# The order on TensorE of a fused attention and expert kernel: the two transposes of a chunk put side by side, and the last batch's projection put behind the scores

## What is computed

```python
def _fastmax_causal_p1(q, k, v):
    qn = max over tokens of |q|;  kn = max over tokens of |k|     # one number each for a head
    q = q / qn;  k = k / kn
    kv = jnp.cumsum(k[..., :, None] * v[..., None, :], axis=2)
    num = jnp.cumsum(v, axis=2) + jnp.einsum('bhnd,bhnde->bhne', q, kv)
    ksum = jnp.cumsum(k, axis=2)
    den = jnp.arange(1, n + 1) + jnp.einsum('bhnd,bhnd->bhn', q, ksum)
    return num / den[..., None]

xn = _layernorm(x)
out = x + attention(xn, Wq, Wk, Wv) @ Wo.T + bo + sum of 2 of 8 experts of xn: (silu(xn @ gate) * (xn @ up)) @ down
```

## Time and profile before

| | |
|---|---|
| median of 3 runs | 1246.61 us (1245.76 to 1248.01) |
| profiled execution, its own time | 1249.39 us |
| its span, first to last instruction | 1247.6 us |
| PE busy | 1162.6 us, 93% of the span, 24462 matmuls |
| DVE busy | 900.1 us, 72% |
| ACT busy | 718.6 us, 58% |
| POOL busy | 325.4 us, 26% |
| chain that ended last | PE 81%, DVE 8%, issue 3%, DMA 3%, POOL 3%, ACT 1% |
| mean granted TensorE clock | 0.981 of full speed |

### The profile page before, as it was taken

One profiled execution on the slowest core, in us unless ns is written; L12 is line 12 of the kernel. 1 busy time (PEld: TensorE's weight loads), 2 busy tenths in 40 slices (PEclk: granted clock), 3 DMA queues, 4 the chain that ended last, 5 costly groups with the idle time before them and its releaser, 6 DMA issues.

```text
span 1247.6 us, 58621 instructions
## 1 busy us (share of the span) xinstructions
PE 1162.6 (93%) x24462; PEld 1037.9 (83%) x24463; DVE 900.1 (72%) x2518; ACT 718.6 (58%) x1707; POOL 325.4 (26%) x461
## 2 busy tenths in 40 slices
PE   6899999999999999999999999998979999999990
PEld 5688888878887888888788878887869999999980
DVE  6888778877887887788788778877873444444446
ACT  5666566646765565656476566746544555555550
POOL 4000111111111111111111111231572555555550
PEclk9999999999999999999999999999998999999995
DMA  7000000000000000000000000002245777777779
GB/s 244 1 4 6 12 12 12 14 12 12 15 12 11 15 14 12 12 15 13 12 14 15 12 12 15 14 25 59 72 115 191 263 273 263 272 262 267 268 258 378
DMA packets 59943, 109.40 MB, mean 88 GB/s; under 512 B 9072, under 2 KB 30192, under 8 KB 59728
## 3 DMA queue, kind: packets, MB, share of 16 engines
q1 hardware_dynamic: 49216, 82.80, 19.3%
q0 software_dynamic: 9216, 19.19, 4.7%
q10 hardware_dynamic: 1296, 4.19, 0.8%
HBM read 28.94 MB, written 24.58 MB: 43 GB/s over the span
## 4 chain that ended last, share of the span: by engine, by line
PE 81%; DVE 8%; issue 3%; DMA 3%; POOL 3%; ACT 1%; SPq 0%; POOLq 0%; DVEq 0%; ACTq 0%
PE bank L1250 12%; PE bank L1252 10%; PE bank L1251 10%; PE bank L1536 8%; PE bank L1424 8%; PE bank L1350 6%; PE bank L1402 5%; PE bank L1289 4%; PE bank L1387 4%; PE bank L1376 4%; PE bank L1336 3%; PE bank L1413 2%; DVE qs L850 2%; PE bank L1368 1%; PE bank L1516 1%
## 5 line engine op out<-in xcount | busy, mean ns | idle before, releaser
L1219 DVE TENSOR_TENSOR aT<-bank,aT 128x256 f32<-128x256 f32 (+1 forms) x216 | 91.4, 423 | 148.4 <-ACT aT L771 142.9
L505 POOL COPY xn<-meta 128x2 f32<-128x2 f32 x128 | 26.9, 210 | 655.6 <-PE bank L1387 292.4
L606 POOL DMA_INDIRECT expert_rows<-yt,wdi x144 | 140.2, 973 | 144.5 <-ACT yt L777 121.5
L644 ACT ACTIVATE kn<-bank 128x512 f32<-128x512 f32 x128 | 69.5, 595 | 145.3 <-PE bank L1336 145.2
L1250 PE MATMUL bank<-xTh,Wh 128*128 128x256 f32 x512 | 152.4, 298 | 0.6 <-DVE xs L844 0.6
L662 ACT ACTIVATE qs<-qs,cvec 128x128 f32<-128x128 f32 x480 | 146.1, 395 | 0.2 <-DVE cvec L899 0.2
L1251 PE MATMUL bank<-xTh,Wl 128*128 128x256 f32 x512 | 145.6, 284 | 0.0
L1252 PE MATMUL bank<-xTl,Wh 128*128 128x256 f32 x512 | 145.4, 284 | 0.0
L509 POOL DMA_INDIRECT sorted_tokens<-xn,slot x128 | 124.7, 974 | 52.1 <-POOL xn L505 49.6
L1250 PEld LDWEIGHTS bank<-xTh,Wh 128*128 128x128 f32 x512 | 98.5, 192 | 47.8 <-issue 44.7
L1250 PE MATMUL bank<-xtTh,cw 128*128 128x256 f32 (+1 forms) x432 | 134.3, 311 | 2.1 <-issue 2.1
(11 more groups left out here) (216 smaller groups left out, 2687.2 us busy)
## 6 DMA issues: line engine op xcount, KB each, us to landing
cw<-guh SPq DMA_DIRECT2D x73, 352.0 KB
cw<-gul SPq DMA_DIRECT2D x73, 352.0 KB
xt<-sorted_tokens SPq DMA_DIRECT2D x73, 132.0 KB, 2.3
er<-expert_rows SPq DMA_DIRECT2D x15, 512.0 KB, 7.7
xa<-in_x SPq DMA_DIRECT2D x8, 512.0 KB, 10.9
out<-xa ACTq DMA_DIRECT2D x7, 512.0 KB, 8.2
gu<-in_gate_up_w SPq DMA_DIRECT2D x8, 352.0 KB, 3.3
expert_rows<-yt,wdi POOLq DMA_INDIRECT x144, 2.5
```

The lines of the kernel that those rows point to most:

```text
L606: pool.indirect_dma_start(ys_d, bass.IndirectOffsetOnAxis(ap=wdi[:, q:q + 1], axis=0), yt[:, q, :], None).then_inc(f_sc[q], 16)
L1219: last = dve.tensor_tensor(a_, bank[1 + FT * s + t][0:k, W:2 * W], a_, ALU.mult)
```

## The change

TensorE's round in batches 0 to 6 is reordered: the head turn stands behind the norms, the key turn right behind the head turn, and both ahead of the fills (before: the key turn between outer products and scores, the head turn behind fills and logits). In the last batch the projection of the chunk before moves from ahead of the outer products to behind the scores (and the rank matmul), and the key turn behind the head turn. The list of bank jobs follows. On ScalarE the copies of both turns move behind the scaling and the normalising, ahead of the squares; on VectorE `attended` moves behind the mask in the last batch alone. Chunk 7 of batches 0 to 6 keeps its order. No instruction is added or removed but for line numbers, which move by up to 2.

```diff
@@ psum_order
-                if c > 0:
+                if c > 0 and more:
                     yield ("O", g - 1)
                 if g + 1 < C:
                     yield from uses_D(g + 1)
-                if g + 2 < C:
-                    yield from uses_KT(g + 2)
                 if c == 0:
                     yield from uses_S(g + 1)
                 if c < CB - 2:
                     yield from uses_S(g + 2)
                 if c == rank_at(b):
                     yield ("R", b)
+                if c > 0 and not more:
+                    yield ("O", g - 1)
+                if c > 0 and more:
+                    yield from uses_norm(G - 1 + c % 2, 1 - c % 2)
+                yield from uses_T(g)
+                if g + 2 < C:
+                    yield from uses_KT(g + 2)
                 if more:
-                    if c > 0:
-                        yield from uses_norm(G - 1 + c % 2, 1 - c % 2)
                     yield from uses_fills(G, c % 2)
                     if c % 2 == 0:
                         yield from uses_logits(G)
-                yield from uses_T(g)
@@ scalar
-                if c > 0:
-                    heads_out(g - 1)
...
-                if g + 2 < C:
-                    keys_out(g + 2)
                 if c + 3 < CB:
                     scale_q(b, c + 3)
...
+                heads_out(g)
+                if g + 2 < C:
+                    keys_out(g + 2)
                 if more:
                     for f in range(4):
                         square(G, 4 * (c % 2) + f)
@@ vector
-                if c > 0:
+                if c > 0 and more:
                     attended(g - 1)
...
                 if c == rank_at(b):
                     place_rows(b)
+                if c > 0 and not more:
+                    attended(g - 1)
@@ tensor
-                if c > 0:
+                if c > 0 and more:
                     project(g - 1)
                 if g + 1 < C:
                     outer(g + 1)
-                if g + 2 < C:
-                    keys(g + 2)
                 if c == 0:
                     scores(g + 1)
                 if c < CB - 2:
                     scores(g + 2)
                 if c == rank_at(b):
                     rank(b)
+                if c > 0 and not more:
+                    project(g - 1)
+                if c > 0 and more:
+                    norms(G - 1 + c % 2, 1 - c % 2)
+                turn(g)
+                if g + 2 < C:
+                    keys(g + 2)
                 if more:
-                    if c > 0:
-                        norms(G - 1 + c % 2, 1 - c % 2)
                     for f in range(4):
                         fill(G, 4 * (c % 2) + f)
                     if c % 2 == 0:
                         logits(G)
-                turn(g)
```

More of the change, by code:

```diff
@@ L760, in tile_hi @@
                 act.activation(xtTh[:, s, :], src[:, 0:W], ACT.Copy).then_inc(f_xTh, 1)
-            heads_out(C - 1)
             tile_hi(0, 0, pbank("tile"))
```

## The result

| | before | changed |
|---|---|---|
| median of 20 runs each, us | 1246.99 | 1249.87 |
| ratio, 95% interval | 1 | 1.0027 (1.0016 to 1.0037) |
| profiled execution, us (span) | 1249.39 (1247.6) | 1252.82 (1251.0) |
| spread to spread, mean of seven batches, us | 113.48 | 113.83 |
| last spread to first tile transposes, us | 86.45 | 89.03 |

What follows compares the result with a forecast made beforehand. TensorE (PE) was taken to set the pace, with almost no idle time. Seams in chunks 0 to 5 win 13.0 us, chunk 6 costs 6.8, the last batch 0: 6.2 less, 1240.4 us, range 1234 to 1247.5.

Steps and rivals of the forecast that it cites:

- the price of the seams: Chunks 0 to 5 of batches 0 to 6: joining groups of one array shape on PE wins 0.31 us a chunk.
- Rival 3: Joined groups of one shape still drain, nothing is won and chunk 6 costs its 6.8 us: 1253.4; chance 0.10.
- VectorE's idle fifth takes that up, and each chunk meets PE again at the projection: Chunks 0 to 5: fills and VectorE's copies start 0.35 us later against the outer products, absorbed by VectorE's idle time.
- chunks 6 and 7: Key turn waits 0.55 us for the value sums' bank; fills and VectorE's chain come 1.05 us late; 6.8 us in all.
- over 2 us at the norms of chunk 7: Sign that the forecast is right: PE waits over 2 us at these norms, where it waited 1.24 before.
- Rival 4: PE's clock falls for part of each batch because two turns stand together; up to 16 us a batch lost; chance 0.01.
- I count 0: Last batch: earlier heads and later projection about cancel for GpSimd's start behind the places; bounds 0.5 us either way.
- So only what moves 879.23 counts: Last batch: its end hangs on GpSimd, which waits for the places until 879.23 and then works without a pause.
- 0.6 us of cover: Last batch: the last head turn moves from 931.94 to near 934.7, leaving 0.6 us before 935.97 once run.
- rival 2: Last batch: late low parts of weights and head turn, or GpSimd's projection waits, lose 2 to 5 us; chance 0.18.

Runs made afterwards that it cites:

- e3: Changed kernel, but in chunk 3 of batches 0 to 6 VectorE does the second half of the places ahead of the copies of the fills; 1241.11 us.
- e6: Changed kernel, but in chunk 6 of batches 0 to 6 the value sums' bank goes to the second fill, not the key turn; 1246.92 us.
- e2: Changed kernel, but chunk 6 of batches 0 to 6 keeps the old order (key turn ahead of norms, head turn behind logits); 1240.5 us.
- e1: Changed kernel, but the last batch has the order of before; 1247.82 us.
- e7: Changed kernel, but in chunks 5 and 6 of the last batch ScalarE makes the weights' high parts ahead of its head and key copies; 1247.20 us.

## Why the prediction was wrong

**Right: the price of the seams.** Against 0.31 us a chunk the joined groups gave 0.35 where nothing else came up, within the bounds of 0 and 0.37; the five chunks without a new wait won 1.52 of 1.55 us a batch, the pauses included. Rival 3 (the seams stay) fell.

**Wrong: chunk 4.** The step that failed is the sentence "VectorE's idle fifth takes that up, and each chunk meets PE again at the projection". An idle share of VectorE over a batch says nothing of the stretch from the fills of chunk 3 to the heads of chunk 4, in which the rows of before show no gap, 8.9 us, and 0.3 us to spare. The forecast looked at how late the fills come after the outer products (0.35 us). What counts is the distance from the fills to the *next* outer products, and that lost the whole head turn, 0.64 us. The wait cost 0.65 us a batch, 4.6 us in seven; with the pauses that stand in chunk 4 in three batches it is 0.88 against the forecast, 6.2 us: as much as all of the gain that was forecast. e3, which changes nothing but VectorE's order, shows it: 8.8 us less, and no wait at these outer products. No rival named it.

**Right in kind and size: chunks 6 and 7.** Forecast was 1.05 us a batch, in a key turn that waits 0.55 and fills that shift VectorE's chain. The key turn came 0.54 us late, which less the seam that the turns won is a loss of 0.45, and the norms of chunk 7 lost 0.65, together 1.10; e6 and e2 show both parts. (The sign "over 2 us at the norms of chunk 7" does not follow from that sum: 1.05 less the 0.55 at the key turn leaves 1.24 + 0.50 = 1.74 there; measured were 1.89.) Here I had followed VectorE's chain row by row; in chunk 4 I had not.

**Put at nothing: the clock.** Rival 4 had a fall of the clock with a chance of 0.01, since "the rounds stay as dense as they are". That holds for the joined turns of chunks 0 to 5, where no fall shows, but not for chunk 7, whose wait ahead of the norms grew from 1.24 to 1.89 us. There the clock fell in three batches, 4.7 us in the profile; the estimate over all executions is 2.5 us.

**Wrong: the end.** "I count 0" for the places was right (29.21 us for 29.71). What failed is "So only what moves 879.23 counts", and the step on ScalarE: it moved only the second four high parts behind a later copy, and found 0.6 us of cover. But the first four moved too, behind the copies of chunk 5's heads and keys, which wait for turns that now stand behind scores and projection, and through VectorE they make the head turn late for which the second four wait; and the tile load on SyncE waits for the low parts, a queue that the sum left out. It cost 2.6 us; rival 2 named the late low parts, with 2 to 5 us. e1 and e7 show it.

Against the forecast, then, by the profile: 6.2 us in chunk 4, 2.4 in chunks 6 and 7 (0.35 x 7: the clock's 4.7, less the 2.4 by which the pauses in the heads of chunk 6 went down, and small terms), 2.6 at the end; smaller differences ahead of the first batch and in the experts go the other way.

## What to carry to other kernels

When a group moves on the engine that sets the pace, take for each neighbour engine the stretch between the two places where it meets that engine, and ask what the move adds to or takes from that stretch on the pacing engine; an idle share over a whole batch covers nothing. Joining neighbours of one array shape is worth about 0.17 us a join here, but only in an order that lets the long chains start as early as before: turns at the end, or turns in the middle with the other engine's spare work moved into the gap. Price a longer wait on the pacing engine for its clock, too: here it fell in chunk 7 only in the kernels that wait longest there. And follow the queues that copy and load (here ScalarE's copies of weights and SyncE's first load) past every group that moves.

## What the runs showed that was not expected

The waits that the profile puts to "issue" have a cause in the trace. Of those between 75 and 850 us, 15 in the changed kernel (without the seven at the key turn of chunk 6) and 11 before, each one ends 1.2 to 1.6 us after a packet of the instruction queue has landed. For the second piece of the scores of chunk 2 in batch 2, timeline of PE after:

```profile
322.25 0.39 PE L1352 MATMUL bank<-qs,ks 64*64 64x64 f32 x10 [0.26 <-issue]
```

and the DMA queues in the stretch from 319 to 321 us (queue and kind: packets, MB, share), in which this one packet starts at 319.99 and takes 0.93 us:

```profile
q8 instruction: 1, 0.02, 2.9%
```

Most fall into the long runs of short matmuls, and a new order moves them: before they stood mostly in the heads, after the change in the scores, with the turns at the end in the heads again and more of them (15.5 us in 16 pieces, against 10.7 in 10). As means over seven batches, the heads of chunks 1 and 2 became 0.44 and 0.36 us shorter by the change, and the scores of chunks 0 and 2 0.37 and 0.36 longer. The Trainium skill ("Runtime: NRT & Kernel Launch", Instruction fetch mechanics) says that an engine fetches its instructions in blocks of 16 KB, 256 instructions, and that the cost of crossing a block is mostly hidden. The packets here have that size; hidden they are in most places, but not in runs of matmuls that start every 0.016 us. That the fetch causes these pauses is read from the times alone; no run took it away.
